# Second expert layer: deeper lead of transposes and first products, and one PSUM bank and one rectifying engine per tile

## Chip, cores, metric

One core of a Trainium2 chip runs the whole program. The metric is the device time of one execution in microseconds (us); lower is better. The kernel before takes 1164.05 us (median of three runs, 1163.82 to 1165.67).

## What is computed

A small language tower in fp32: token embedding and value embedding of 8 x 500 tokens (width 128), then two layers, each a mixer (a long convolution, then an attention) followed by a mixture of experts. The change touches the expert layers, the second one above all. Its reference, cut to the core:

```python
h = h + _L1_ffn_ref(_layernorm(h), g1, g2, W1, b1, W2, b2)

def _L1_ffn_ref(x, g1, g2, W1, b1, W2, b2):     # x: 4000 tokens x 128
    # two groups of 8, then two experts of 8 in each: four of 64 experts for a token
    # c1, c2: softmax weights of the picks
    h = relu(einsum('td,gedh->tgeh', xt, W1) + b1)      # 128 -> 256
    y = einsum('tgeh,gehd->tged', h, W2) + b2           # 256 -> 128
    out = sum over the picks of c1 * c2 * y
```

The first expert layer is of the same form with 8 experts, two picks for a token and a middle layer of 512.

## The kernel before

**Routing.** Only the picked experts are computed. Token rows are sorted by expert and cut into blocks of 128. A table on the chip names, for each tile of work, a block and an expert; a block that holds rows of several experts is worked several times. The second layer (`FFN[1]`, `c.n == 1`) has 125 blocks, 64 experts and so 188 tiles; the first (`c.n == 0`) has 63 blocks and 70 tiles. The program is written out for all tiles, with expert numbers and places of blocks read from the table into registers (`Words`, a load for every two tiles, line 420).

**A tile** has these steps, each on one engine, tied by semaphores that count up:

- POOL gathers the 128 rows of a block from DRAM into one of eight places (`RING`), line 871. Gather j waits until block j - 8 has been transposed (`turned`). There are 125 gathers, one for a block.
- PE transposes the block (`turn`, line 634) into bank `u % 2` of PSUM; DVE copies it to SBUF (line 507, semaphore `blocks_in`).
- DVE copies the tile's expert weights and bias from `big` into one of four places (`stage`, line 504, semaphore `w1_ready`).
- PE makes the first products (`first`, line 639): two chunks (`HC` = 2) of 128 columns. Chunk 0 goes to bank 2 + u % 2, chunk 1 to bank 4 + u % 2.
- ACT rectifies chunk 0 (line 606), DVE chunk 1 (line 512), both into `hid[u % 2]`.
- PE makes the second products (`second`, line 646) into bank 6 + u % 2 once both semaphores, `hid_dve` and `hid_act`, are there.
- ACT copies the result out (line 624), SP stores two tiles at a time to DRAM (line 481).

**Order on PE** in iteration u: transpose of u + 2, first products of u + 1, second products of u. Transposes stop after block 124; from then on the blocks are in SBUF and an iteration holds products only. On DVE: copy of transpose u + 2, rectify u + 1, stage weights of u + 3. On ACT: rectify u + 1, copy result u. PE's waits in an iteration with a transpose are the row's landing, `blocks_in`, `hid_dve` and `hid_act`; without a transpose they are `w1_ready`, `hid_dve` and `hid_act`, and once in eight tiles (line 675) `blocks_in` as well. Every fp32 matmul shows in the trace as two, so four MATMUL records stand for the two products of a step.

**Around it.** POOL has two more sets of gathers, of result rows that are added up for each token. The first 32 (line 884) may start before the layer's end: after DVE has worked out, at tile 156 (`stores_needed`, lines 533 to 541, in front of it `lower_places` at tile 144), how many stores they need, and after those stores have landed. The other 96 (line 949) wait for all results (`results_in`, line 494); from the ninth on each waits for an addition by DVE (line 1309), which in turn follows the late gates (lines 1227 to 1245), eight bias products (lines 2149 and 2156) and the bias's addition (line 998).

Of the kernel before, what the change touches and what calls it, by code (L numbers as in the profile page):

```python
# [25 lines left out]
D = 128  # L26
# [15 lines left out]
class Ffn:  # L42


    def __init__(self, n, groups, experts, picks, hidden, wide, w1, b1, w2, b2):
# [6 lines left out]
        self.full = (self.blocks - 2) // RING  # L52
# [80 lines left out]
def tower_kernel(nc, a, out):  # L133
# [15 lines left out]
    with ExitStack() as ctx:  # L149
# [200 lines left out]
        class Ring:  # L350

            def __init__(self, c):
# [10 lines left out]
                self.rows, self.hid = take(RING, 128), take(2, 128 * c.HC)  # L363
                self.res = take(RING, 128)
# [85 lines left out]

        def store_rows(sp, c):

            sp.wait_ge(S(f"x{c.n + 1}_act"), B if c.n else B // 2)
            if c.n == 0:
                sp.wait_ge(S("x1_dve"), B // 2)
            for lo, hi in ((0, 112), (112, R)):
                sp.dma_start(xrows[:, :].rearrange("(p t) d -> p (t d)", p=R)[lo:hi], xbuf[lo:hi, :]).then_inc(S(f"x{c.n + 1}_st"), 16)

        def expert_dma(sp, c):
# [31 lines left out]
            sp.wait_ge(S(p + "w1_ready"), c.tiles + 5)  # L491
            sp.wait_ge(S(p + "hid_dve"), c.tiles + 3)
            sp.wait_ge(S(p + "hid_act"), c.tiles + 3)
            sp.sem_inc(S(p + "results_in"), 1)  # L494

        def expert_vector(dve, c, me):
# [3 lines left out]
            half = c.HC // 2  # L500
# [5 lines left out]
            def turn(u, kept):  # L506
                v.tensor_copy(ring.blocks[:, bass.ds(kept, 128)], ps[:, u % 2, 0:128]).then_inc(S(p + "blocks_in"), 1)  # L507

            def rectify(u):
                w = ring.w1[u % U]  # L510
                for k in range(half, c.HC):
                    last = v.tensor_scalar(ring.hid[u % 2][:, 128 * k:128 * k + 128], ps[:, 4 + u % 2, 128 * k:128 * k + 128],  # L512
# [45 lines left out]
            dve.sem_inc(S(p + "hid_dve"), 2)  # L558
            dve.wait_ge(S(f"w{c.n}_ld"), 16 * weight_loads(c))
            w1, _ = pairs_of(mybir.EngineType.DVE, stage_table, 0, 2, (c.E - 1) * c.wcols, (KEEP[c.n] - 1) * 128)  # L560
            words = Words(dve, p, stage_table, 2, (c.E - 1) * c.wcols, (KEEP[c.n] - 1) * 128)
            dve.wait_ge(S("bank_filled"), nfill[at[f"holder{c.n}", 0]])
            stage(0, 0)
            dve.wait_ge(S(p + "turned"), 1)
            v.tensor_copy(ring.blocks[:, 0:128], ps[:, 0, 0:128]).then_inc(S(p + "blocks_in"), 1)
            stage(w1[0], 1)
            dve.wait_ge(S(p + "turned"), 2)
            v.tensor_copy(ring.blocks[:, 128:256], ps[:, 1, 0:128]).then_inc(S(p + "blocks_in"), 1)
            stage(w1[1], 2)
            dve.wait_ge(S(p + "hid_filled"), 3)  # L570
            rectify(0)

            def tiles(first_tile, count, turns):
# [17 lines left out]
            tiles(c.full * RING, RING, c.blocks - 2 - c.full * RING)  # L591
# [6 lines left out]
        def expert_scalar(act, c):  # L598

            p, ring, s = f"f{c.n}_", Ring(c), nc.scalar  # L600
            half, hid = c.HC // 2, 128 * c.HC

            def rectify(u):
                w = ring.w1[u % U]
                for k in range(half):
                    last = s.activation(ring.hid[u % 2][:, 128 * k:128 * k + 128], ps[:, 2 + u % 2, 128 * k:128 * k + 128],  # L606
                                        ACT.Relu, bias=w[:, hid + k:hid + k + 1])
                last.then_inc(S(p + "hid_act"), 1)
            act.sem_inc(S(p + "hid_act"), 2)
# [7 lines left out]
            def tiles(first_tile, count):  # L617
                for u in range(count):
                    act.wait_ge(S(p + "hid_filled"), first_tile + (u + 4))
                    rectify(u + 1)  # L620
# [8 lines left out]
        def expert_tensor(pe, c):  # L629
# [3 lines left out]
            def turn(u):  # L633
                t.transpose(ps[:, u % 2, 0:128], ring.rows[u % RING], ident).then_inc(S(p + "turned"), 1)  # L634

            def first(u, kept):
                turned = ring.blocks[:, bass.ds(kept, 128)]
                for k in range(c.HC):
                    last = t.matmul(ps[:, (2 if k < c.HC // 2 else 4) + u % 2, 128 * k:128 * k + 128], ring.w1[u % U][:, 128 * k:128 * k + 128],  # L639
                                    turned, start=True, stop=True)  # L640
                last.then_inc(S(p + "hid_filled"), 1)

            def second(w2, u):
                w = w2v[:, bass.ds(w2, c.HC * D)]
                for k in range(c.HC):
                    last = t.matmul(ps[:, 6 + u % 2, 0:D], ring.hid[u % 2][:, 128 * k:128 * k + 128],  # L646
# [3 lines left out]
            words = Words(pe, p, tile_table, 0, (c.E - 1) * c.HC * D, (KEEP[c.n] - 1) * 128)  # L650
            pe.sem_inc(S(p + "hid_filled"), 2)
            pe.sem_inc(S(p + "res_filled"), 2)
            pe.wait_ge(S("row_ld0"), 16 + earlier_rows(c, 0))
            turn(0)
            pe.wait_ge(S("row_ld1"), 16 + earlier_rows(c, 1))
            turn(1)
            pe.wait_ge(S(p + "w1_ready"), 3)
            pe.wait_ge(S(p + "blocks_in"), 1)
            first(0, 0)
# [3 lines left out]
            def tiles(first_tile, count, turns):  # L663
# [1551 lines left out]
```

## Time and profile before

| what | value |
|---|---|
| median of 3 runs | 1164.05 us |
| span of the profiled execution, first to last instruction | 1254.4 us |
| PE busy | 737.2 us (59%) |
| DVE busy | 748.9 us (60%) |
| ACT busy | 406.2 us (32%) |
| POOL busy | 536.2 us (43%) |
| granted TensorE clock, mean | 0.721 of 2.4 GHz |

The profiled execution's own time is told by its span alone; it is 90 us longer than the median of the runs, so not every stretch of the trace lasts as long in a run as it does here. A row of the page's groups or of a stretch's groups gives line, engine, operation, tiles, count, busy time and mean of one, and after the bar the idle time ahead of it with what ended it. A row of the timeline gives start, length, engine, line, operation, count and in brackets the idle time before it. A row of windows gives busy time and count (x) of each engine, the granted clock, DMA share and GB/s.

### The profile page before, as it was taken

Reading aid. Unit: us, or ns where it says so; the run is one execution under the profiler, and the core shown is the slowest. Engines: PE = TensorE matmul, PEld = TensorE weight load, DVE = VectorE, ACT = ScalarE, POOL = GpSimd, SP = SyncE. Lnnn points to the kernel's source line nnn. Section 1 sums busy time; section 2 is a strip of 40 time slices with the busy share of each in tenths; the row PEclk is TensorE's granted clock in tenths of the full one; section 3 lists DMA queues with packets and bytes.
Section 4 is the critical chain, followed back from the end, with each engine's and each line's share of the span. In section 5 each row is a group of like instructions: output and inputs, shape, how many; then the busy total and the mean of one; then the engine's idle time right before and its main releaser. Section 6 shows DMA issues by size and latency. Waiting matters only on the chain.

```text
span 1254.4 us, 16064 instructions
## 1 busy us (share of the span) xinstructions
PE 737.2 (59%) x4622; PEld 585.6 (47%) x4622; DVE 748.9 (60%) x2175; ACT 406.2 (32%) x1123; POOL 536.2 (43%) x562
## 2 busy tenths in 40 slices
PE   0205966669999237878597413577777894452000
PEld 0205355559999214434255401366666894442000
DVE  6896174856666318788776799555555552275222
ACT  2274151524444133433102306533333462220000
POOL 8853000245450645563100005756666306347664
PEclk9657975559999656676665655589999997665555
DMA  2390049502221266657500404033333222112221
GB/s 67 113 388 1 1 143 320 173 24 68 71 72 42 58 119 127 142 124 137 94 0 1 129 0 138 23 83 85 88 86 88 77 64 66 53 43 77 63 54 52
DMA packets 113503, 111.45 MB, mean 89 GB/s; under 512 B 15891, under 2 KB 99922, under 8 KB 113170
## 3 DMA queue, kind: packets, MB, share of 16 engines
q1 hardware_dynamic: 100172, 83.36, 24.5%
q0 software_dynamic: 13248, 27.06, 8.4%
q8 instruction: 42, 0.69, 0.2%
q14 instruction: 41, 0.34, 0.1%
HBM read 76.08 MB, written 34.26 MB: 88 GB/s over the span
## 4 chain that ended last, share of the span: by engine, by line
PE 46%; DVE 30%; issue 10%; another core or an unknown queue 6%; ACT 3%; DMA 2%; POOL 1%; SPq 1%; DVEq 0%; ACTq 0%; POOLq 0%
PE ps L639 13%; PE ps L646 12%; DVE wide L1330 6%; DVE h L1309 5%; PE ps L1896 4%; PE ps L634 2%; DVE bnst L964 2%; DVE wide L1208 2%; PE ps L2066 2%; PE ps L2107 2%; PE ps L2156 1%; ACT wide L1694 1%; PE ps L2046 1%; DVE mv L967 1%
## 5 line engine op out<-in xcount | busy, mean ns | idle before, releaser
L871 POOL DMA_INDIRECT wide<-xrows,holder x188 | 180.1, 958 | 137.5 <-PE ps L634 91.1
L639 PE MATMUL ps<-wide 128*128 (+1 forms) x1324 | 205.9, 288 | 42.6 <-issue 25.4
L646 PE MATMUL ps<-big,wide 128*128 x1312 | 196.2, 282 | 40.3 <-issue 21.7
L639 PEld LDWEIGHTS ps<-wide 128*128 128x128 f32 x1324 | 174.7, 198 | 56.2 <-issue 53.3
L646 PEld LDWEIGHTS ps<-big,wide 128*128 128x128 f32 x1312 | 171.8, 196 | 43.7 <-issue 43.6
L512 DVE TENSOR_SCALAR wide<-ps,wide 128x128 f32<-128x128 f32 x331 | 109.2, 348 | 129.5 <-PE ps L639 78.6
L1330 DVE TENSOR_REDUCE wide<-ps 125x3 f32<-125x1500 f32 (+1 forms) x96 | 143.7, 1540 | 46.4 <-PE ps L1896 44.4
L606 ACT ACTIVATE wide<-ps,wide 128x128 f32<-128x128 f32 x331 | 114.0, 366 | 169.8 <-PE ps L639 132.9
L1896 PE MATMUL ps<-big 97*125 97x500 bf16 x256 | 105.4, 548 | 40.3 <-DVE wide L1330 33.0
L949 POOL DMA_INDIRECT wide<-results,place x96 | 95.8, 998 | 68.2 <-SPq L494 26.8
L862 POOL TENSOR_SCALAR wide<-tileno,sm 125x128 f16<-125x128 f16 x64 | 40.8, 644 | 168.4 <-DVE sm L1195 143.9
L624 ACT COPY wide<-ps 128x128 f32<-128x128 f32 x258 | 68.4, 265 | 114.9 <-PE ps L646 82.2
L507 DVE COPY wide<-ps 128x128 f32 x184 | 53.4, 290 | 80.2 <-PE ps L634 67.6
L504 DVE COPY wide<-big 128x258 f32 (+2 forms) x264 | 87.0, 330 | 3.9 <-issue 3.8
L905 POOL DMA_INDIRECT wide<-results,place x64 | 61.0, 954 | 60.6 <-SPq L494 34.3
L1896 PEld LDWEIGHTS ps<-big 97*125 97x125 bf16 x256 | 42.9, 193 | 88.6 <-DVE wide L1330 51.2
L2156 PE MATMUL ps<-b,cst 8*125 8x128 f32 (+1 forms) x128 | 33.0, 435 | 75.4 <-issue 70.5
L1309 DVE SCALAR_TENSOR_TENSOR h<-wide,big,h 125x128 f32<-125x128 f32 x96 | 32.7, 351 | 74.6 <-DVE h L1309 24.7
L2156 PEld LDWEIGHTS ps<-b,cst 8*125 8x125 f32 (+1 forms) x128 | 28.3, 322 | 81.3 <-issue 72.3
L2046 PE MATMUL ps<-cst,wide 125*128 125x125 f32 x96 | 22.4, 390 | 62.8 <-ACT wide L1694 62.7
L634 PE MATMUL ps<-cst,wide 128*128 128x128 f32 x188 | 53.4, 285 | 7.2 <-DMA wide<-xrows,holder 4.6
L884 POOL DMA_INDIRECT big<-results,place x32 | 30.4, 950 | 58.5 <-DMA results<-wide 49.1
(384 smaller groups left out, 1197.2 us busy)
## 6 DMA issues: line engine op xcount, KB each, us to landing
results<-wide SPq DMA_DIRECT2D x129, 128.0 KB, 1.8
big<-kappa SPq DMA_DIRECT2D x8, 1750.0 KB, 21.4
big<-parts SPq DMA_DIRECT2D x96, 125.0 KB
big<-in_L_ffn_W_dram SPq DMA_DIRECT2D x10, 1024.0 KB, 9.6
big<-in_L_ffn_W_dram SPq DMA_DIRECT2D x64, 128.0 KB, 2.7
parts<-wide SPq DMA_DIRECT2D x24, 250.0 KB
xrows<-wide SPq DMA_DIRECT2D x2, 1792.0 KB
wide<-xrows,holder POOLq DMA_INDIRECT x188
```

The lines of the kernel that those rows point to most:

```text
L504: v.tensor_copy(ring.w1[u % U], w1v[:, bass.ds(w1, c.wcols)]).then_inc(S(p + "w1_ready"), 1)
L512: last = v.tensor_scalar(ring.hid[u % 2][:, 128 * k:128 * k + 128], ps[:, 4 + u % 2, 128 * k:128 * k + 128], w[:, hid + k:hid + k + 1], 0. ...
L606: last = s.activation(ring.hid[u % 2][:, 128 * k:128 * k + 128], ps[:, 2 + u % 2, 128 * k:128 * k + 128], ACT.Relu, bias=w[:, hid + k:hid ...
L634: t.transpose(ps[:, u % 2, 0:128], ring.rows[u % RING], ident).then_inc(S(p + "turned"), 1)
L639: last = t.matmul(ps[:, (2 if k < c.HC // 2 else 4) + u % 2, 128 * k:128 * k + 128], ring.w1[u % U][:, 128 * k:128 * k + 128], turned, sta ...
L646: last = t.matmul(ps[:, 6 + u % 2, 0:D], ring.hid[u % 2][:, 128 * k:128 * k + 128], w[:, D * k:D * k + D], start=k == 0, stop=k == c.HC - 1)
L871: gp.indirect_dma_start(ring.rows[j % RING], None, xrows[:, :], bass.IndirectOffsetOnAxis(ap=holder[:, j:j + 1], axis=0)).then_inc(S(f"row ...
L949: gp.indirect_dma_start(got[m % 8], None, results[f][:, :], bass.IndirectOffsetOnAxis(ap=place[f][:, k, t:t + 1], axis=0)).then_inc(S(f"go ...
L1309: v.scalar_tensor_tensor(h[:, t, :], rows[0:R, :], swapped_gate[:, k, t:t + 1], h[:, t, :], ALU.mult, ALU.add).then_inc(S("f1_combined"), 1)
L1330: v.tensor_reduce(out=mcol[:, j, H * b + lo:H * b + hi], in_=ps[0:R, 3 * (n % 2):3 * (n % 2) + hi - lo, 0:L], axis=AX.X, op=ALU.max).then_ ...
L1896: last = t.matmul(ps[0:R, 3 * (n % 2) + head - lo, 0:L], stack[0:SROWS, 0, b % 2, head, R * j:R * j + R], stack[0:SROWS, 1, b % 2, head, : ...
L2156: last = t.matmul(p[0:R, D * j:D * j + D], cT[0:c.E, R * j:R * j + R], b2[0:c.E, f, :], start=True, stop=True)
```

## The change

For the second layer alone (`c.n == 1`; the first keeps its numbers):

- transposes run four tiles ahead instead of two (`lead`), first products two instead of one (`ahead`), staged weights five instead of three (`stages`, still four places, so DVE waits for the rectification of tile u + 1 before it stages u + 5);
- a tile's two chunks go to one bank, 2 + u % 4, and are rectified by one engine: ACT for even tiles, DVE for odd ones, into four places instead of two;
- PE waits for one rectification semaphore instead of two, and in addition for `res_ready` (the result copy two tiles back) and, in each iteration, for `blocks_in` and `w1_ready`;
- in the first layer PE waits for `blocks_in` and `w1_ready` in each iteration.

```diff
+        self.ahead = 2 if n else 1
+        self.lead = 4 if n else 2
+        self.stages = 5 if n else 3
+        self.slots = 4 if n else 2
...
+                if c.n:
+                    self.hid += [cst[:, 128 + 256 * i:384 + 256 * i] for i in range(2)]
...
+        def middle(c, u, k):
+            n = 2 + u % 4 if c.n else (2 if k < c.HC // 2 else 4) + u % 2
+            return ps[:, n, 128 * k:128 * k + 128]
+
+        def halves(c, u, engine):
+            if c.n:
+                return range(c.HC) if engine == ("act", "dve")[u % 2] else range(0)
+            return range(c.HC // 2) if engine == "act" else range(c.HC // 2, c.HC)
...
+        def wait_rectified(eng, c, u):
+            for engine in (("act", "dve")[u % 2],) if c.n else ("dve", "act"):
+                eng.wait_ge(S(f"f{c.n}_hid_{engine}"), rectified(c, u, engine))
...
                     if u < turns:
-                        dve.wait_ge(S(p + "turned"), first_tile + (u + 3))
-                        turn(u, words.value(u, 1))
-                    dve.wait_ge(S(p + "hid_filled"), first_tile + (u + 4))
-                    rectify(u + 1)
-                    stage(words.value(u, 0), u + 3)
+                        dve.wait_ge(S(p + "turned"), first_tile + (u + c.lead + 1))
+                        turn(u + c.lead, words.value(u, 1))
+                    if first_tile + u + c.ahead < c.tiles and halves(c, u + c.ahead, "dve"):
+                        dve.wait_ge(S(p + "hid_filled"), first_tile + (u + c.ahead + 3))
+                        rectify(u + c.ahead)
+                    if first_tile + u + c.stages < c.tiles:
+                        if c.stages > U:
+                            wait_rectified(dve, c, first_tile + u + c.stages - U)
+                        stage(words.value(u, 0), u + c.stages)
...
                 for u in range(count):
+                    n = u + c.lead
+                    if c.n and first_tile + u + c.ahead < c.tiles:
+                        pe.wait_ge(S(p + "blocks_in"), min(first_tile + (u + c.ahead + 1), c.blocks))
                     if u < turns:
-                        pe.wait_ge(S(f"row_ld{(u + 2) % RING}"), (first_tile + (u + 2) // RING * RING) * (16 // RING) + 16 + earlier_rows(c, u + 2))
-                        turn(u + 2)
-                        pe.wait_ge(S(p + "blocks_in"), first_tile + (u + 2))
-                    if u >= turns:
-                        pe.wait_ge(S(p + "w1_ready"), first_tile + (u + 4))
-                    if u == turns:
-                        pe.wait_ge(S(p + "blocks_in"), c.blocks)
-                    first(u + 1, words.value(u, 1))
-                    pe.wait_ge(S(p + "hid_dve"), first_tile + (u + 3))
-                    pe.wait_ge(S(p + "hid_act"), first_tile + (u + 3))
+                        pe.wait_ge(S(f"row_ld{n % RING}"), (first_tile + n // RING * RING) * (16 // RING) + 16 + earlier_rows(c, n))
+                        turn(n)
+                    if first_tile + u + c.ahead < c.tiles:
+                        if c.n == 0:
+                            pe.wait_ge(S(p + "blocks_in"), min(first_tile + (u + c.ahead + 1), c.blocks))
+                        pe.wait_ge(S(p + "w1_ready"), first_tile + (u + c.ahead + 3))
+                        first(u + c.ahead, words.value(u, 1))
+                    wait_rectified(pe, c, first_tile + u)
+                    if c.n:
+                        pe.wait_ge(S(p + "res_ready"), first_tile + (u + 1))
                     second(words.value(u, 0), u)
```

## Rows read from the trace of the kernel before

**Rows 1.** The page's first line: span and instructions.
```profile
span 1254.4 us, 16064 instructions
```
**Rows 2.** Windows: busy time and count of PE, PEld, DVE, ACT, POOL; clock, DMA.
```profile
300.00:400.00 100.00, 100.00 (x899) 100.00 (x898) 64.52 (x209) 47.02 (x159) 39.66 (x43) 1.00 0.23 65
...
823.00:1003.00 180.00, 137.72 (x1087) 126.68 (x1087) 96.34 (x360) 69.91 (x242) 104.95 (x110) 0.99 0.31 85
1003.00:1041.00 38.00, 37.09 (x290) 33.80 (x288) 22.75 (x92) 22.51 (x72) 0.00 (x0) 1.00 0.22 64
...
1107.00:1244.00 137.00, 24.37 (x96) 18.50 (x96) 55.17 (x136) 4.55 (x8) 94.96 (x96) 0.51 0.22 58
```
**Rows 3.** Timeline beside gathers, 883 to 886 us, cut.
```profile
883.17 0.61 PE L646 MATMUL ps<-big,wide 128*128 x4
...
885.62 0.27 ACT L624 COPY wide<-ps 128x128 f32<-128x128 f32 x1 [1.08 <-PE ps L646]
885.75 0.29 DVE L507 COPY wide<-ps 128x128 f32 x1 [0.88 <-PE ps L634]
```
**Rows 4.** Timeline of POOL: four row gathers one after another.
```profile
881.32 0.94 POOL L871 DMA_INDIRECT wide<-xrows,holder  x1 [1.15 <-PE ps L634]
882.56 0.94 POOL L871 DMA_INDIRECT wide<-xrows,holder  x1 [0.30 <-issue]
883.81 0.94 POOL L871 DMA_INDIRECT wide<-xrows,holder  x1 [0.30 <-issue]
885.88 0.94 POOL L871 DMA_INDIRECT wide<-xrows,holder  x1 [1.14 <-PE ps L634]
```
**Rows 5.** Line 634 from 803 to 1003 us: duration min/median/max, first and last start.
```profile
L634 PE MATMUL ps<-cst,wide x125: 272/273/476, 803.6 to 998.6; 128*128 128x128 f32 x125
```
**Rows 6.** Timeline, the last row gather, and two late transposes.
```profile
991.05 0.95 POOL L871 DMA_INDIRECT wide<-xrows,holder  x1 [1.23 <-remote]
...
997.58 0.27 PE L634 MATMUL ps<-cst,wide 128*128 128x128 f32 x1
...
998.58 0.27 PE L634 MATMUL ps<-cst,wide 128*128 128x128 f32 x1
```
**Rows 7.** Timeline, 1041 to 1088 us, cut: engines that wait beside result gathers.
```profile
1075.80 0.27 ACT L624 COPY wide<-ps 128x128 f32<-128x128 f32 x1 [9.45 <-remote]
...
1084.20 0.35 DVE L512 TENSOR_SCALAR wide<-ps,wide 128x128 f32<-128x128 f32 x1 [17.68 <-remote]
```
**Rows 8.** Lines from 830 to 990 us: DVE's three operations of a tile.
```profile
L512 DVE TENSOR_SCALAR wide<-ps,wide 128x128 f32<-128x128 f32 x104 | 36.2, 348 | 16.7 <-PE ps L639 11.3 <-issue 1.8
L504 DVE COPY wide<-big 128x258 f32 x104 | 30.8, 296 | 0.1
L507 DVE COPY wide<-ps 128x128 f32 x104 | 30.2, 290 | 60.3 <-PE ps L634 53.8 <-issue 4.0 <-remote 0.7
```
**Rows 9.** Timeline after the transposes: four second products in a row.
```profile
1010.23 0.64 PE L646 MATMUL ps<-big,wide 128*128 x4
...
1011.35 0.61 PE L646 MATMUL ps<-big,wide 128*128 x4
...
1012.24 0.64 PE L646 MATMUL ps<-big,wide 128*128 x4
...
1013.47 0.61 PE L646 MATMUL ps<-big,wide 128*128 x4
```
**Rows 10.** Line 481 to 1037.5 us: stores of two tiles, first and last issue.
```profile
L481 SPq DMA_DIRECT2D results<-wide x79: 359/360/367, 817.6 to 1037.0; - x79
```
**Rows 11.** Timeline: first of the 32 early result gathers.
```profile
1041.04 0.95 POOL L884 DMA_INDIRECT big<-results,place  x1 [49.05 <-DMA results<-wide]
```
**Rows 12.** Timeline after the layer: late gates, first and ninth of the last gathers.
```profile
1105.38 1.95 DVE L1227 TENSOR_TENSOR wide<-sm,em 125x512 f32<-125x512 f32 x4
...
1107.73 1.15 POOL L949 DMA_INDIRECT wide<-results,place  x1 [26.84 <-SPq L494]
...
1124.69 1.00 POOL L949 DMA_INDIRECT wide<-results,place  x1 [3.90 <-DVE h L1309]
```

More of the change, by code:

```diff
@@ L449, in late_place, with turned_at, rectified, wait_all_rectified @@
             return 16 * (m // 8) + 8 + m % 8 if m < 8 * EARLY else 8 * EARLY + m
+        def turned_at(u):
+            return ps[:, u % 2, 0:128]
+        def middle(c, u, k):
[5 more added lines that the diff above has]
+            return range(c.HC // 2) if engine == "act" else range(c.HC // 2, c.HC)
+        def rectified(c, u, engine):
+            return u // 2 + 1 if c.n else u + 3
+        def wait_rectified(eng, c, u):
+            for engine in (("act", "dve")[u % 2],) if c.n else ("dve", "act"):
+                eng.wait_ge(S(f"f{c.n}_hid_{engine}"), rectified(c, u, engine))
+        def wait_all_rectified(eng, c):
+            for u in range(c.tiles - 2, c.tiles) if c.n else (c.tiles - 1,):
+                wait_rectified(eng, c, u)
         def store_rows(sp, c):
@@ L506, in turn @@
             def turn(u, kept):
-                v.tensor_copy(ring.blocks[:, bass.ds(kept, 128)], ps[:, u % 2, 0:128]).then_inc(S(p + "blocks_in"), 1)
+                v.tensor_copy(ring.blocks[:, bass.ds(kept, 128)], turned_at(u)).then_inc(S(p + "blocks_in"), 1)
             def rectify(u):
                 w = ring.w1[u % U]
-                for k in range(half, c.HC):
-                    last = v.tensor_scalar(ring.hid[u % 2][:, 128 * k:128 * k + 128], ps[:, 4 + u % 2, 128 * k:128 * k + 128],
+                for k in halves(c, u, "dve"):
+                    last = v.tensor_scalar(ring.hid[u % c.slots][:, 128 * k:128 * k + 128], middle(c, u, k),
                                            w[:, hid + k:hid + k + 1], 0.0, ALU.add, ALU.max)
@@ L590, in expert_vector @@
                 tiles(i * RING, RING, RING)
-            tiles(c.full * RING, RING, c.blocks - 2 - c.full * RING)
+            tiles(c.full * RING, RING, c.blocks - c.lead - c.full * RING)
             if c.tiles // RING > c.full + 1:
@@ L618, in tiles @@
                 for u in range(count):
-                    act.wait_ge(S(p + "hid_filled"), first_tile + (u + 4))
-                    rectify(u + 1)
+                    if first_tile + u + c.ahead < c.tiles and halves(c, u + c.ahead, "act"):
+                        act.wait_ge(S(p + "hid_filled"), first_tile + (u + c.ahead + 3))
+                        rectify(u + c.ahead)
                     act.wait_ge(S(p + "res_filled"), first_tile + (u + 3))
@@ L633, in turn @@
             def turn(u):
-                t.transpose(ps[:, u % 2, 0:128], ring.rows[u % RING], ident).then_inc(S(p + "turned"), 1)
+                t.transpose(turned_at(u), ring.rows[u % RING], ident).then_inc(S(p + "turned"), 1)
             def first(u, kept):
@@ L638, in first @@
                 for k in range(c.HC):
-                    last = t.matmul(ps[:, (2 if k < c.HC // 2 else 4) + u % 2, 128 * k:128 * k + 128], ring.w1[u % U][:, 128 * k:128 * k + 128],
-                                    turned, start=True, stop=True)
+                    last = t.matmul(middle(c, u, k), ring.w1[u % U][:, 128 * k:128 * k + 128], turned, start=True, stop=True)
                 last.then_inc(S(p + "hid_filled"), 1)
@@ L645, in second @@
                 for k in range(c.HC):
-                    last = t.matmul(ps[:, 6 + u % 2, 0:D], ring.hid[u % 2][:, 128 * k:128 * k + 128],
+                    last = t.matmul(ps[:, 6 + u % 2, 0:D], ring.hid[u % c.slots][:, 128 * k:128 * k + 128],
                                     w[:, D * k:D * k + D], start=k == 0, stop=k == c.HC - 1)
                 last.then_inc(S(p + "res_filled"), 1)
-            words = Words(pe, p, tile_table, 0, (c.E - 1) * c.HC * D, (KEEP[c.n] - 1) * 128)
+            if c.ahead > 1:
+                _, kept = pairs_of(mybir.EngineType.PE, tile_table, 0, c.ahead - 1, (c.E - 1) * c.HC * D, (KEEP[c.n] - 1) * 128)
+            words = Words(pe, p, tile_table, c.ahead - 1, (c.E - 1) * c.HC * D, (KEEP[c.n] - 1) * 128)
             pe.sem_inc(S(p + "hid_filled"), 2)
             pe.sem_inc(S(p + "res_filled"), 2)
[L653 to L659, printed above, removed]
+            for u in range(c.lead):
+                pe.wait_ge(S(f"row_ld{u}"), 16 + earlier_rows(c, u))
+                if u >= 2:
+                    pe.wait_ge(S(p + "blocks_in"), u - 1)
+                turn(u)
+            for u in range(c.ahead):
+                pe.wait_ge(S(p + "w1_ready"), u + 3)
+                pe.wait_ge(S(p + "blocks_in"), u + 1)
+                first(u, kept[u - 1] if u else 0)
             if c.n:
@@ L683, in expert_tensor @@
                 tiles(i * RING, RING, RING)
-            tiles(c.full * RING, RING, c.blocks - 2 - c.full * RING)
+            tiles(c.full * RING, RING, c.blocks - c.lead - c.full * RING)
             if c.tiles // RING > c.full + 1:
@@ L880, in _ @@
                     pool.wait_ge(S("early_known"), 2)
-                    pool.wait_ge(S(q + "w1_ready"), LOWER_AT + 6)
+                    pool.wait_ge(S(q + "w1_ready"), LOWER_AT + c.stages + 3)
                     for b in range(EARLY):
@@ L2182, in _ @@
                 pe.wait_ge(S(q + "res_ready"), c.tiles + 2)
[L2183 to L2184 removed]
+                wait_all_rectified(pe, c)
                 if f == 0:
```

50 lines of the change are left out of this document (27 added, 23 removed).

## The prediction

> **What bounds the kernel now.** I read the page first, then windows over the stages, then the timeline of the second expert layer engine by engine, and POOL's timeline beside it.
>
> The page's span is 90 us longer than the median of the runs [rows 1]; something in the trace isn't in the runs. So the first question is what in this layer is real. In the windows the first expert layer is full: PE is busy for 100 of 100 us [rows 2]. The second isn't: from 823 to 1003 us PE is busy for 137.7 of 180 us [rows 2]. The 125 transposes start over 195 us, 1.57 us apart [rows 5].
>
> The timeline says where that time goes. Second products start at 883.17 us and by their length end at 883.78, but ACT, which waits for nothing else of them, copies their result at 885.62, and DVE gets the next transpose only at 885.75 [rows 3]. Every third tile or so PE's end is told 1.5 to 2 us late while PE goes on issuing. It happens beside gathers: POOL issues three 1.25 us apart, then waits for PE [rows 4]. After the last gather, at 991.05 us, transposes follow each other in 1.00 us with no such hold [rows 6]. And while POOL issues the 32 early result gathers without a pause (from 1041.04 us [rows 11]), ACT waits 9.45 us and DVE 17.68 us for PE [rows 7]. I call these holds.
>
> Are the holds in the runs? Take them out. The transposes then go at the pace of the gathers, 1.25 us, in 125 x 1.25 = 156 us instead of 195: 39 us less. The early gathers then start at 1041 - 39 = 1002 us, take 32 x 1.25 = 40 us and end at 1042. The layer's last 28 tiles take 1105.4 - 1041.0 = 64 us in the trace against 28 x 1.02 = 29 us without holds [rows 9, 11, 12], so it ends before POOL is through, and the 26.8 us for which POOL waits at 1107.73 us [rows 12] go too. Together 66 us of the 90 that the trace is too long. I therefore take the holds as things of the profiled execution. The Trainium skill, "NOTIFIC — the notification-queue block", section 7.1, says that the block's internal pipeline always presses back on its producers rather than lose a record, which would let recording throttle an engine; rows 3 and 7 look like that, and no row proves it.
>
> So in a run the layer is bound by POOL: row gathers at 1.25 us, PE with about 1.0 us of work in each of them [rows 4, 6]. After the last gather PE has the rest to do at 1.02 us a tile. The 32 early gathers start when the stores of their tiles have landed: the 79th store, tiles 156 and 157, is issued at 1037.0 us and POOL starts at 1041.04 [rows 10, 11]. From there POOL's 32 + 96 gathers lead to the end: in the last stretch POOL is busy for 95 of 137 us, with pauses of 0.30 us between [rows 2]. What the change does counts up to tile 157's store.
>
> **The change part by part.**
>
> *Deeper lead while rows are gathered.* Nothing. Tile 1.25 us, PE 1.0 us, DVE 0.290 + 0.348 + 0.296 = 0.93 us [rows 8] on average, also when it rectifies both chunks of every second tile. The new waits add at most 0.11 us a tile on PE (below), 1.11 < 1.25. Cover: the gather. If the gather were faster than 1.11 us, PE would bound both kernels and the waits would cost up to 0.06 x 120 = 7 us.
>
> *The lead itself costs at the end of the gathers.* The order on PE is fixed: transpose u + 4, first products u + 2, second products u. When transpose 124 arrives, the kernel before stands at second products 122, the new one at 120. Both get it at the same time, so 2 tiles more lie behind it: 2 x 1.02 = +2.0 us.
>
> *More waits on PE's queue after the transposes.* Before, an iteration there has `w1_ready` and two waits for the rectified halves; once in eight tiles `blocks_in` is added. Second products start at 1010.23, 1011.35, 1012.24 and 1013.47 us: 1.12, 0.89 and 1.23 us [rows 9]. The long ones hold the load of registers for two tiles (line 420), after which PE starts its next product late; the 1.23 is the tile with the added wait for `blocks_in`. One wait more right behind a register load costs 0.11 us; in the other tile of a pair it is hidden, 0.89 being eight matmuls without a gap. The new kernel has that wait in each iteration (the wait for `res_ready` takes the place of one for a half). So 3 of 4 pairs become 0.11 us longer: 0.041 us a tile, over 37 tiles (120 to 157) +1.5 us. Queued behind each such wait are the first products of u + 2, and behind them everything on PE. Bounds: 0, if two waits share an instruction, and 0.11 x 37 = +4.1 us.
>
> *What the lead saves there.* The pattern gives (3 x 2.01 + 2.12)/8 = 1.02 us a tile. The window 1003 to 1041 us has 290 matmul records, 36.3 tiles, in 38 us: 1.05 us [rows 2]. The excess, about 1.0 us, holds DVE's side work at tiles 144 and 156, for which PE waits; a lead of two tiles covers a part. I take -0.7 us; bounds -1.4 and 0.
>
> *One bank and one engine for a tile.* Rectification of a tile takes 0.70 us instead of 0.35, off the path: between first products u and second products u lie more than a tile and a half of PE work, 1.5 us. DVE's new wait, for tile u + 1's rectification before it stages u + 5, has behind it that copy and the next transpose's copy; ACT has been through with u + 1 for a tile. 0 us; bounds 0 and +1.
>
> *Start of the layer.* First products wait for four transposes instead of two, 2.5 us at 1.25 us a row. The eight places for rows give POOL room until its ninth gather, 10 us in, so POOL is not held. 0 us; bounds 0 and +2.5.
>
> *First layer.* `w1_ready` is waited for in each iteration. PE is busy for 100 of 100 us [rows 2], register loads included, so its queue runs ahead by more than a wait. 0 us; bound 0.11 x 35 pairs = +3.9 us.
>
> *Registers and end of the layer.* Some loads more at the start, three weight copies of DVE less at the end: nothing. Behind tile 157 the new kernel's slower tiles are covered by the early gathers. The ninth last gather follows the late gates by 1124.69 - 1105.38 = 19.3 us [rows 12]; without holds the layer ends at about 1105.4 - 39 - 35 = 1031, so that chain is at 1051, and POOL at 1042 + 8 x 1.25 = 1052. A margin of 1 to 3 us, from which the slower tiles could add another 28 x 0.041 = 1.1 us.
>
> Sum: 2.0 + 1.5 - 0.7 = +2.8 us. Against the profiled execution's own time that is 1254.4 + 2.8; but there the holds are, and a longer lead hides them, so its span may well fall. The runs don't have them, so I add to their median: 1164.05 + 2.8 = 1166.9 us.
>
> **The rivals.**
>
> *A: the holds are in the runs as well.* For it: they are what the rows show. Against it: the 66 of 90 us above. Three tiles take 4.6 us [rows 4]; a tile more in flight lets PE work 1.0 us longer through each hold, down to the gathers' 3 x 1.25 = 3.75 us. Gain 0.85 us in each of 40 groups, 34 us: 1130. If a fifth of them is real, 7 - 3 = 4 us: 1160. This decides if a fifth or more of the excess in the transposes' stretch is real.
>
> *B: no difference.* The waits share instructions or the queue hides them, DVE's side work is covered, and the 2.0 us of the lead are partly won back since PE can make up the lag in tiles where it now waits: 1164 to 1166.
>
> *C: PE is held by its queue.* If gathers in a run take 1.1 us or less, PE's waits bind among the transposes too, and show in the first layer: 2.8 + 3 to 7 us: 1170 to 1174. It decides from a gather pace below 1.11 us. Against it: with 253 gathers of this layer 0.14 us faster, the runs would be 35 us shorter than I make them.
>
> **How the numbers follow.** A measurement tells about 0.2%, 2.3 us, from no change. My forecast (+1 to +4.5 us around +2.8) has 0.60, of which 0.38 lies above 2.3 us; B 0.15; A 0.17, 0.05 for the full gain and 0.12 for a fifth or so, of which 0.01 falls within 2.3 us; C 0.08, nearly all above. That makes faster 0.16, same 0.38, slower 0.46. The likeliest is the forecast, 1166.9. Range: 1158 to 1171.5, which leaves out A's full gain with a bit of its small one, and half of C. It is wide below, as a share of holds weighs more than any other cost.
>
> **What would show it.** In the new kernel's trace: transposes' starts 1.25 us apart or more and the holds still there beside gathers; the stretch after the last gather with pairs of second products of 2.12 us instead of 2.01; 68 second products behind the last transpose instead of 66; DVE never late for its stagings. I would be wrong if the runs fell by 5 us or more (A), if pairs became shorter than 2.01 us after the transposes, or if PE's share in the first layer fell below 100 of 100.

## The result, and the profile after

The changed kernel takes 1168.92 us (median of 13 runs, 1163.59 to 1173.58) against 1164.05 for the kernel before (13 runs, 1161.38 to 1167.03): ratio 1.0043, 95% interval 1.003 to 1.0056. That is +4.9 us; the forecast was +2.8.

One thing must be known to read the numbers: the kernel before has two levels, which differ between the chips on which the comparisons ran. On one of them all 29 runs of the kernel before took 1256 to 1266 us, near the 1254.4 us of the profile shown ahead of the prediction; on the others they took 1159 to 1168. So each time below stands beside that of the kernel before on its own chip, and for a trace of before at the lower level I profiled the kernel before again (first experiment).

The page's first line, after:

```profile
span 1166.3 us, 16260 instructions
```

Windows of after (columns as in [rows 2]): first layer, the stretch from the last transpose to the 79th store, and the late gathers:

```profile
300.00:400.00 100.00, 100.00 (x899) 100.00 (x898) 64.19 (x208) 47.16 (x159) 38.57 (x41) 1.00 0.23 64
...
944.40:989.20 44.80, 39.43 (x308) 35.69 (x309) 22.45 (x93) 20.06 (x77) 0.00 (x0) 1.00 0.20 57
...
1036.00:1156.00 120.00, 21.00 (x84) 15.91 (x82) 48.49 (x134) 3.98 (x7) 90.74 (x97) 0.50 0.25 67
```

The clock is at its upper level, 2.4 GHz (1.00), in the whole stretch that changed. Two lines fix that stretch: the 125 transposes and the 79 stores that the early gathers wait for, each with first and last start. After, and below them the first early gather:

```profile
L674 PE MATMUL ps<-cst,wide x125: 272/299/476, 788.9 to 944.4; 128*128 128x128 f32 x125
L510 SPq DMA_DIRECT2D results<-wide x79: 359/359/367, 796.9 to 989.2; - x79
...
991.90 0.95 POOL L930 DMA_INDIRECT big<-results,place  x1 [50.47 <-DVE wide L531]
```

The same of the kernel before at the lower level:

```profile
L634 PE MATMUL ps<-cst,wide x125: 272/273/476, 786.2 to 942.8; 128*128 128x128 f32 x125
L481 SPq DMA_DIRECT2D results<-wide x79: 359/360/367, 793.1 to 981.3; - x79
...
985.38 0.94 POOL L884 DMA_INDIRECT big<-results,place  x1 [44.47 <-DVE wide L504]
```

The whole difference of the two spans, 1166.3 - 1159.7 = 6.6 us, can be read here. The last transpose starts 1.6 us later (944.4 against 942.8). From it to the 79th store it is 44.8 us instead of 38.5: +6.3. From the store to the first early gather, 2.7 instead of 4.1: -1.4. From there to the end, 174.4 instead of 174.3: +0.1. So the change is in one stretch, in which PE works alone. I call it the lead-out, and it is a better measure than the time, since in the three kernels profiled twice it repeats within 0.1 us:

| kernel | lead-out, us | time, us | before, same chip | ratio and 95% interval |
|---|---|---|---|---|
| before | 38.5 | | | |
| after | 44.8 | 1168.92 | 1164.05 | 1.0043 [1.003, 1.0056] |
| after, again | 44.8 | 1171.96 | 1165.48 | 1.0054 [1.0039, 1.007] |
| aligned | 35.1 | 1160.09 | 1163.79 | 0.9966 [0.9949, 0.9982] |
| aligned, again | 35.1 | 1161.72 | 1165.48 | 0.9963 [0.9948, 0.9977] |
| aligned, fewer waits | 35.1 | 1159.20 | 1163.79 | 0.9956 [0.9938, 0.9973] |
| before, table 8 bytes on | 49.1 | 1189.65 | 1163.79 | 1.0206 [1.018, 1.0232] |
| before, table 16 bytes on | 38.5 | 1257.61 | 1260.25 | 0.9979 [0.9964, 0.9994] |
| before, more waits | 40.2 | 1262.28 | 1260.25 | 1.0011 [0.9994, 1.0027] |
| one tile ahead | 41.3 | 1265.45 | 1260.25 | 1.0048 [1.0032, 1.0064] |
| aligned, lead 3, stagings 5 | 34.5 | 1252.45 | 1260.25 | 0.9942 [0.9926, 0.9957] |
| lead 3, stagings 4 | 37.6 | 1164.24 | 1165.48 | 0.9982 [0.9967, 0.9998] |
| the same, fewer waits | 35.4 | 1158.75 | 1165.48 | 0.9952 [0.9936, 0.9968] |

What fills the lead-out? PE's timeline of after, second products on L685:

```profile
970.32 0.71 PE L679 MATMUL ps<-wide 128*128 x4 [0.31 <-issue]
970.86 0.61 PE L685 MATMUL ps<-big,cst 128*128 x4
971.31 0.61 PE L679 MATMUL ps<-wide 128*128 x4
971.76 0.61 PE L685 MATMUL ps<-big,cst 128*128 x4
972.65 0.71 PE L679 MATMUL ps<-wide 128*128 x4 [0.28 <-issue]
```

A pair of tiles takes 972.65 - 970.32 = 2.33 us, where four products back to back (0.45 us each) would take 1.79. The gap stands once a pair, behind the second of its two second products, and no other engine is named for it ("issue"). What the code has there, once a pair, is the load of four words from the tile table into PE's registers. Its line in the trace, after (L426, PE's queue and DVE's; then PE's in the first layer), shows it:

```profile
L426 PEldq TENSOR_LOAD <-tile_table x88: 997/1040/1207, 800.1 to 1013.8; - x88
L426 DVEq TENSOR_LOAD <-stage_table x86: 341/346/354, 800.9 to 1009.9; - x86
...
L426 PEldq TENSOR_LOAD <-tile_table x35: 327/332/527, 271.4 to 392.9; - x35
```

and before:

```profile
L420 PEldq TENSOR_LOAD <-tile_table x86: 327/332/376, 801.0 to 1003.6; - x86
```

PE's load takes 1.04 us where it took 0.33; DVE's and the first layer's are unchanged. The load is the same four words. What the diff does to it: `Words` gets `c.ahead - 1` = 1 as its first index instead of 0, and the table is written one pair of words further on, so each of PE's loads in the second layer starts 8 bytes further. Places are counted here from the start of the table; where the table itself lies in memory no trace tells.

### The profile page after: what moved, and what is told of

The parts are those of the page before. It is cut to its first block, busy times and chain, and to the rows that moved or that the text cites. A ratio compares the mean times of both kernels' runs of the same rounds, so it can differ in the third digit from the quotient of the medians.

```text
span 1166.3 us, 16260 instructions
## 1 busy us (share of the span) xinstructions
PE 726.1 (62%) x4610; PEld 574.6 (49%) x4610; DVE 748.1 (64%) x2166; ACT 391.2 (34%) x1120; POOL 536.7 (46%) x562
## 4 chain that ended last, share of the span: by engine, by line
PE 43%; DVE 28%; POOL 10%; issue 7%; DMA 7%; ACT 4%; SPq 1%; DVEq 0%; POOLq 0%; ACTq 0%
PE ps L679 11%; PE ps L685 10%; DVE wide L1376 7%; POOL wide L995 4%; PE ps L1942 4%; DMA wide<-results,place 3%; POOL big L930 3%; DVE bnst L1010 3%; DVE wide L1254 3%; PE ps L2112 3%; PE ps L674 2%; ACT wide L1740 2%; PE ps L2153 2%; POOL wide L917 2%; PE ps L2202 1%
## 5 line engine op out<-in xcount | busy, mean ns | idle before, releaser
L679 PE MATMUL ps<-wide 128*128 (+1 forms) x1312 | 200.0, 285 | 9.2 <-issue 8.5
L679 PEld LDWEIGHTS ps<-wide 128*128 128x128 f32 x1312 | 169.5, 194 | 16.1 <-issue 15.1
L685 PE MATMUL ps<-big,wide 128*128 x936 | 131.9, 276 | 0.0
L685 PEld LDWEIGHTS ps<-big,wide 128*128 128x128 f32 x936 | 118.2, 193 | 0.2 <-issue 0.2
L644 ACT ACTIVATE wide<-ps,wide 128x128 f32<-128x128 f32 x234 | 73.1, 363 | 114.5 <-PE ps L679 113.7
L539 DVE TENSOR_SCALAR wide<-ps,wide 128x128 f32<-128x128 f32 x234 | 71.4, 347 | 62.1 <-PE ps L679 60.5
L995 POOL DMA_INDIRECT wide<-results,place x96 | 91.3, 951 | 29.3 <-issue 24.4
L531 DVE COPY wide<-big 128x258 f32 (+3 forms) x258 | 84.5, 335 | 4.1 <-issue 4.0
L951 POOL DMA_INDIRECT wide<-results,place x64 | 60.8, 949 | 50.7 <-SPq L522 33.7
L685 PE MATMUL ps<-big,cst 128*128 x376 | 57.4, 275 | 0.2 <-issue 0.2
L2213 PE MATMUL ps<-wide 125*128 125x128 f16 x192 | 28.5, 303 | 41.3 <-DVE wide L1254 39.7
```

The costliest lines, as they stand in the source:

```text
L531: v.tensor_copy(ring.w1[u % U], w1v[:, bass.ds(w1, c.wcols)]).then_inc(S(p + "w1_ready"), 1)
L539: last = v.tensor_scalar(ring.hid[u % c.slots][:, 128 * k:128 * k + 128], middle(c, u, k), w[:, hid + k:hid + k + 1], 0.0, ALU.add, ALU.max)
L644: last = s.activation(ring.hid[u % c.slots][:, 128 * k:128 * k + 128], middle(c, u, k), ACT.Relu, bias=w[:, hid + k:hid + k + 1])
L679: last = t.matmul(middle(c, u, k), ring.w1[u % U][:, 128 * k:128 * k + 128], turned, start=True, stop=True)
L685: last = t.matmul(ps[:, 6 + u % 2, 0:D], ring.hid[u % c.slots][:, 128 * k:128 * k + 128], w[:, D * k:D * k + D], start=k == 0, stop=k == c ...
L995: gp.indirect_dma_start(got[m % 8], None, results[f][:, :], bass.IndirectOffsetOnAxis(ap=place[f][:, k, t:t + 1], axis=0)).then_inc(S(f"go ...
```

## The experiments

**First comparison: what is in the runs, and is it the place of the load?** The kernel before, unchanged.

> The kernel before, profiled once more, unchanged. If the long holds of PE's ends beside gathers belong to that one profiled execution, this one has none: span about 1162 us, row gathers 1.25 us apart from first to last (156 us), pairs of second products 2.01 us after the last transpose, the early result gathers starting about 39 us earlier against the last row gather than in the first trace. If the holds belong to the kernel and only the change took them away, the span is again about 1254 us.

Measured: 1161.5 us, span 1159.7, transposes 1.26 us apart, no holds. Its gathers, to compare with [rows 4]:

```profile
879.31 0.94 POOL L871 DMA_INDIRECT wide<-xrows,holder  x1 [0.30 <-issue]
880.56 0.94 POOL L871 DMA_INDIRECT wide<-xrows,holder  x1 [0.30 <-issue]
881.80 1.00 POOL L871 DMA_INDIRECT wide<-xrows,holder  x1 [0.30 <-issue]
```

Against the 1254.4 us shown ahead, the transposes' stretch is 38.4 us shorter (156.6 instead of 195.0), the first transpose 17.4 us earlier, the lead-out the same (38.5 and 38.4), the rest 39.0 us shorter.

*aligned*: the changed kernel with the second layer's tile table 8 bytes further on, so that PE's loads start where they did.

```diff
-tile_table = sb("tile_table", [1, 2 * TAB], I32)
+tile_words = sb("tile_table", [1, 2 * TAB], I32)
+tile_tables = [tile_words[:, 0:2 * TAB], tile_words[:, 2:2 * TAB]]
...
-words = Words(pe, p, tile_table, c.ahead - 1, ...)
+words = Words(pe, p, tile_tables[c.n], c.ahead - 1, ...)
```

> The changed kernel with the second layer's table of tiles moved by one pair of words (8 bytes), so that each of PE's loads of four words starts where it did in the kernel before; nothing else differs. Theory place (the load is slow because the change moved its first word by 8 bytes): loads of registers on PE take 0.33 us instead of 1.0, pairs of second products after the last transpose 2.12 us instead of 2.34, over 37 tiles 4.0 us less, about 1165 us, 0.1% over the kernel before. Theory queue (the load waits for products queued before it, since the longer lead lets PE's queue run further ahead): loads still 1.0 us, pairs 2.34 us, 1169 us, 0.4% over.

Measured: 1160.09 us, 3.7 under before; more than I expected, since the pairs are not 2.12 us but 1.79. Load, lead-out window and timeline:

```profile
L427 PEldq TENSOR_LOAD <-tile_table x87: 327/332/561, 801.8 to 996.3; - x87
...
942.90:978.00 35.10, 35.10 (x314) 34.75 (x313) 21.96 (x92) 20.11 (x77) 0.00 (x0) 1.00 0.26 73
...
960.45 0.61 PE L686 MATMUL ps<-big,cst 128*128 x4
960.89 0.61 PE L680 MATMUL ps<-wide 128*128 x4
961.34 0.61 PE L686 MATMUL ps<-big,wide 128*128 x4
961.79 0.61 PE L680 MATMUL ps<-wide 128*128 x4
```

PE is busy for 35.10 of 35.10 us: a load of 0.33 us is hidden wholly behind queued matmuls. By my sum the waits should have shown here; they don't.

*before_shifted*: the same shift in the kernel before, alone.

> The kernel before with the second layer's table of tiles moved by one pair of words (8 bytes), nothing else. Theory place: loads of registers on PE take 1.0 us instead of 0.33 and pairs after the last transpose grow from 2.01 to 2.3 us or more, over 35 tiles 5 us or more: 1169 us, 0.4% over the kernel before or more; among the row gathers nothing changes, as 1.25 us a tile still covers it. Theory queue: loads stay at 0.33 us and the time at 1164 us.

Measured: 1189.65 us, +25.9, five times the least that I expected.

```profile
L421 PEldq TENSOR_LOAD <-tile_table x87: 996/1000/1008, 800.8 to 1038.5; - x87
...
L635 PE MATMUL ps<-cst,wide x125: 272/299/447, 791.3 to 962.8; 128*128 128x128 f32 x125
...
882.38 0.30 PE L635 MATMUL ps<-cst,wide 128*128 128x128 f32 x1 [0.58 <-issue]
...
885.15 0.30 PE L635 MATMUL ps<-cst,wide 128*128 128x128 f32 x1 [0.49 <-issue]
```

The load is at 1.00 us again, with nothing else changed: place, not lead or waits, makes it slow. My expectation counted only the lead-out, and too little there: it rises by 10.6 us, since pairs take 2.68 us (987.45 - 984.77) and not 2.3. And among the row gathers a pair now takes 885.15 - 882.38 = 2.77 us, more than its two gathers' 2.50, so PE and not POOL bounds the layer: transposes 171.5/124 = 1.38 us apart instead of 1.26, +14.9 us. Together 25.5. The changed kernel escapes this, its transposes still 155.5/124 = 1.25 us apart.

*aligned_fewer_waits*: aligned, with `blocks_in` not waited for behind the last transpose.

```diff
-if c.n and first_tile + u + c.ahead < c.tiles:
+if c.n and first_tile + u + c.ahead < c.blocks + 1:
     pe.wait_ge(S(p + "blocks_in"), ...)
```

> The kernel of run aligned without PE's wait for blocks_in in iterations that need no block later than the last. My term for that wait is 0.11 us for each pair of tiles: pairs go from 2.12 us to 2.01 us, over 34 tiles 1.9 us less than run aligned, about 1163 us. If two waits cost PE no more than one, it is the same as run aligned.

Measured: lead-out 35.1 us, the same; 1159.20 us, its interval overlaps aligned's. With a load of 0.33 us and this lead the wait costs nothing.

**Second comparison: control, and the parts one by one** (the chip with the upper level). *before_shifted16*: the table 16 bytes on instead of 8.

> The kernel before with the second layer's tile table moved by 16 bytes instead of 8, so that each of PE's register loads (four words, 16 bytes) starts at a multiple of 16 bytes again. Control for the 8-byte shift, which gave 1189.65 us and loads of 1.0 us. Theory (the place within 16 bytes decides): loads of 0.33 us, pairs of second products 2.01 us behind the last transpose, 1161 to 1166 us, no difference from before. Rival (any moved or newly routed table makes the load slow, for instance by what else lies near it): loads of 1.0 us, pairs 2.7 us, 1189 us.

```profile
L421 PEldq TENSOR_LOAD <-tile_table x18: 327/332/334, 999.7 to 1035.7; - x18
...
L635 PE MATMUL ps<-cst,wide x125: 272/273/474, 802.3 to 998.1; 128*128 128x128 f32 x125
L482 SPq DMA_DIRECT2D results<-wide x79: 359/360/367, 817.0 to 1036.6; - x79
```

Load 0.33 us, lead-out 38.5: as before. Moving the table costs nothing; moving it by half a load's 16 bytes does. (The expected 1161 to 1166 us was for the lower level; here it is 1257.61 against 1260.25. The interval of the ratio, up to 0.9994, just leaves out no difference; the lead-out doesn't show these 2.6 us, and I have no cause for them.)

*before_more_waits*: the kernel before with `blocks_in` waited for in each iteration behind the last transpose.

```diff
-if u == turns:
+if u == turns or c.n and u > turns:
     pe.wait_ge(S(p + "blocks_in"), c.blocks)
```

> The kernel before with the wait for blocks_in in every iteration behind the last transpose, where it has it once in eight; register loads stay at their place. This measures the term of my forecast by itself. The forecast's reading: 0.11 us in each of 3 of 4 pairs, pairs 2.12 instead of 2.01 us, second products of tiles 122 to 157 in 36.9 + 13 x 0.11 = 38.3 us, time +1.5 us, 1165.5. Rival (the wait is free, as with the deeper lead): pairs 2.01 and the time of before within 0.5 us.

```profile
L634 PE MATMUL ps<-cst,wide x125: 272/273/473, 800.1 to 996.1; 128*128 128x128 f32 x125
L481 SPq DMA_DIRECT2D results<-wide x79: 359/359/367, 811.2 to 1036.3; - x79
...
1005.35 0.61 PE L646 MATMUL ps<-big,wide 128*128 x4
...
1007.48 0.61 PE L646 MATMUL ps<-big,wide 128*128 x4
```

A pair takes 2.13 us, the lead-out 40.2: +1.7 where the forecast's term was +1.5. The time's interval (-0.8 to +3.4 us) can't tell. So the term is right for the kernel from whose rows it was read, and only for that.

*one_ahead*: the changed kernel's banks and turns, the lead undone.

```diff
-self.ahead = 2 if n else 1
-self.lead = 4 if n else 2
-self.stages = 5 if n else 3
+self.ahead = 1
+self.lead = 2
+self.stages = 3
```

> The changed kernel's banks and its one engine per tile, with the lead undone: first products one tile ahead, transposes two ahead, three stagings, as before. PE's first index is 0 again, so its register loads start at a multiple of 16 bytes and should take 0.33 us. This is the other part of the change alone. Theory (the lead of two tiles is what hides the register load, since PE's queue can run ahead only as far as its waits are met): without it a tile's rectification, 0.70 us instead of 0.35, stands within the 0.89 us between its first and second products, the queue can run less far ahead, and pairs take 2.1 to 2.4 us instead of 2.01; second products of tiles 122 to 157 in 38 to 42 us, 1166 to 1171 us. Rival (banks and turns are what shorten the tiles, the lead costs only its two tiles of lag): pairs 1.78 us, 0.89 a tile, no lag, 1157 us.

```profile
L675 PE MATMUL ps<-cst,wide x125: 272/300/477, 805.9 to 1003.9; 128*128 128x128 f32 x125
L510 SPq DMA_DIRECT2D results<-wide x79: 359/360/367, 819.2 to 1045.2; - x79
...
1020.37 0.61 PE L686 MATMUL ps<-big,wide 128*128 x4
1020.82 0.61 PE L680 MATMUL ps<-wide 128*128 x4
1021.33 0.71 PE L686 MATMUL ps<-big,wide 128*128 x4
1022.08 0.71 PE L680 MATMUL ps<-wide 128*128 x4
1022.63 0.61 PE L686 MATMUL ps<-big,cst 128*128 x4
...
L426 DVEq TENSOR_LOAD <-stage_table x18: 434/622/632, 1005.1 to 1043.7; - x18
```

A pair takes 2.26 us, the lead-out 41.3, and the time rises by 5.2 us, as the first theory said. PE's loads are at 0.33 us. (DVE's take 0.62 us here, though their place within 16 bytes is that of the kernel before.) 1.7 of the +2.8 us is the wait, which this kernel has as well; 1.1 is what banks and turns cost without the lead: there is a gap in each tile now (second products start 0.96 and 1.30 us apart instead of 0.89 and 1.12). The trace of all engines fits a late rectification: the two chunks on DVE end at 1021.18 us, and the second products, due at 1021.27 behind the first ones, start at 1021.33. That it costs the 1.1 us is argued, not shown.

*aligned_lead3*: transposes three ahead, one number changed. The stagings stay five ahead, so DVE takes the place of the next tile for each turned block and first products read other rows; the amount and order of work are the same, but what it computes isn't the layer's result. It serves for its times alone.

> The aligned version with transposes three tiles ahead instead of four, first products still two ahead. Behind the last transpose stands one tile less. Theory (each tile of lead costs one tile at the end of the gathers, and nothing before it, since DVE and PE have 0.3 us and more to spare in each gather): tile 157's second products come 33.6 us behind the last transpose instead of 34.5, time 0.9 us less than aligned, 1159.2 us. Rival (the transposes' copy by DVE is late for the first products when only one tile lies between them): gathers' pace stays 1.25 but tiles behind it get gaps of 0.1 to 0.2 us, no gain or up to +2 us, 1160 to 1162.

```profile
L675 PE MATMUL ps<-cst,wide x125: 272/302/476, 803.6 to 999.8; 128*128 128x128 f32 x125
L511 SPq DMA_DIRECT2D results<-wide x79: 359/360/367, 818.4 to 1034.3; - x79
```

Lead-out 34.5 us, 0.6 less than aligned for one tile less of lead (0.9 expected). The lead-outs of two chips are compared here, since those of the kernel before agree on both. Time 7.8 us under before; aligned wasn't run on that chip, so I draw nothing more from the time. This trace also speaks on rival A: its lead is deeper than that of the kernel before, yet its transposes stand 196.2/124 = 1.58 us apart, as before_more_waits' do (196.0/124). POOL's gathers in before_more_waits:

```profile
880.64 0.94 POOL L871 DMA_INDIRECT wide<-xrows,holder  x1 [0.30 <-issue]
882.76 0.94 POOL L871 DMA_INDIRECT wide<-xrows,holder  x1 [1.17 <-PE ps L634]
884.00 0.95 POOL L871 DMA_INDIRECT wide<-xrows,holder  x1 [0.31 <-issue]
885.25 0.95 POOL L871 DMA_INDIRECT wide<-xrows,holder  x1 [0.30 <-issue]
```

The hold of [rows 4] is there, every third gather. It is there in aligned_lead3 too (883.28 and 887.95 us, waits of 1.15 and 1.14 us), so a lead of three tiles doesn't bridge it.

**Third comparison: does it repeat, and is a shorter lead better?** The changed kernel and aligned again, unedited.

> The changed kernel unedited, beside the kernel before on the chip that this comparison gets. The runs so far show two levels of the kernel before: 1164 us, and 1260 us with PE's ends told late beside gathers, in all 29 runs of one comparison. Theory (what the change costs lies behind the last transpose, where nothing is held): pairs of second products 2.34 us, tile 157's second products 44 us behind the last transpose, +4.9 us at either level, ratio 1.004. Rival A of the forecast (a deeper lead lets PE work through a hold), only at the upper level: transposes 1.27 us apart instead of 1.58, 1225 to 1250 us there.

> The changed kernel with its register loads at a multiple of 16 bytes, once more, beside the two shorter leads on the same chip. Theory: 4 us under the kernel before at either level (1160 or 1256), 34.5 us from the last transpose to tile 157's second products. Rival (the gain of 3.7 us was this one chip's): within 1 us of before.

Measured: 1.0054 and 0.9963, lead-outs 44.8 and 35.1 us, at the lower level. Between the two on one chip lie 10.2 us, 9.7 of them in the lead-out. Rival A at the upper level was not tried with the changed kernel itself.

*lead3*: transposes three ahead with the stagings four ahead, DVE's table moved by 8 bytes as well, so that its loads stay at a multiple of 16.

```diff
-self.lead = 4 if n else 2
-self.stages = 5 if n else 3
+self.lead = 3 if n else 2
+self.stages = 4 if n else 3
```

> The aligned version with transposes three tiles ahead and four stagings (its tables laid out for that, so that each transpose goes to its own place). Theory (each tile of lead costs one tile at the end of the gathers and nothing before it): 33.6 us from the last transpose to tile 157's second products instead of 34.5, and 0.9 us less than aligned in the same comparison. Rival (a fourth tile of lead pays for itself while rows are gathered, or staging one tile later makes PE wait for DVE): the last transpose later by 1 us or more, or gaps of 0.1 us and more in the 0.89 us tiles; same time as aligned or above.

> The three-tile lead without the wait for blocks_in behind the last transpose. Theory (with the two-tile lead of first products that wait is hidden behind matmuls, while in the kernel before it cost 0.15 us a pair): same time as lead3 within 1 us, tiles of 0.89 us. Rival (the wait costs 0.11 us in three of four pairs): 1.5 us less than lead3.

```profile
L677 PE MATMUL ps<-cst,wide x125: 272/296/477, 791.4 to 947.7; 128*128 128x128 f32 x125
L512 SPq DMA_DIRECT2D results<-wide x79: 359/359/367, 800.3 to 985.3; - x79
...
966.15 0.61 PE L688 MATMUL ps<-big,cst 128*128 x4
966.67 0.71 PE L682 MATMUL ps<-wide 128*128 x4
...
968.11 0.61 PE L688 MATMUL ps<-big,wide 128*128 x4
```

PE's loads in the two lead-outs, lead3 and then lead3_fewer_waits:

```profile
L428 PEldq TENSOR_LOAD <-tile_table x19: 332/587/606, 948.2 to 983.9; - x19
...
L428 PEldq TENSOR_LOAD <-tile_table x19: 328/342/610, 943.0 to 976.7; - x19
```

Both expectations missed. lead3's lead-out is 37.6 us where 0.9 less than aligned's 35.1 was expected: pairs take 968.11 - 966.15 = 1.96 us with a gap behind the load. Without the wait it is 35.4. So with the stagings four ahead taking out the same wait gives 2.2 us, where with five it gave nothing. The loads tell how: in lead3 they take 0.59 us, at a place where aligned's take 0.33. The load at 965.81 us ends at 966.40, and the next first products start 0.27 us later, at 966.67.

The same holds in every trace in which a gap stands behind a load. From the load's end to the next first products it is 0.27 us with `blocks_in` and `w1_ready` behind the load, 0.16 with `w1_ready` alone. The difference is the forecast's 0.11 us. What is hidden depends on how early the load starts: 0.28 us before the last matmul of the second products ahead of it with first products one tile ahead (before, one_ahead), 0.76 us with two (after, aligned), 0.64 in lead3 (medians in the lead-outs). With matmuls 0.11 us apart, aligned's 0.33 + 0.27 = 0.60 fits into 0.76 + 0.11; after's 1.02 (its median there) + 0.27 = 1.29 and lead3's 0.59 + 0.27 = 0.86 against 0.64 + 0.11 don't.

With a load of 0.33 us lead3 would have no gap by this sum, so it is the load's length that costs. What makes the load longer stays open. aligned_lead3 (stagings five ahead, transposes three: loads 0.33 us, lead-out 34.5) points to the stagings and not the transposes. But it ran on the other chip and with blocks at other places, and lead3 also moves DVE's table, so this is not shown. The times, 1164.24 and 1158.75, lie 5.5 us apart, more than the 2.2: in the two traces the first transpose alone, which no changed wait touches, starts at 791.4 and 786.2 us. lead3_fewer_waits has the lowest ratio at the lower level, 0.9952, but its interval covers aligned's 0.9963.

## Why the prediction was right, and where it was not

The verdict, slower by more than 0.2%, and the range held. The sum did so partly by luck: two of its terms were far off, with opposite signs.

- *Bound and path*: right. POOL's 1.25 us a gather bounds the layer, the lead-out is what the change moves, and behind the first early gather both kernels need 174.3 and 174.4 us. The early gathers start over 43.5 us in both (985.38 to 1028.90 us in before) and not the 40 that I gave them.
- *Holds*: right for the chip of the comparison, wrong as I put it. They are no thing of one profiled execution: on one chip all 29 runs of before are at 1260 us. Of the 94.7 us between the two traces of before, 38.4 and 39.0 lie where I took out 39 and 27; the other 17.4 lie ahead of the layer's transposes, where I had looked for nothing. What makes the holds stays open. The Trainium skill, "NOTIFIC — the notification-queue block", section 7.1, tells how recording could throttle an engine; no run here shows that it does.
- *Deeper lead while rows are gathered, 0*: right, 1.25 us apart. *First layer, 0*: right, PE 100 of 100 us. *Start of the layer, 0*: right, POOL's 125 gathers start over 155.9 us after and 156.4 before.
- *The lead at the end of the gathers, +2.0*: two tiles of 0.89 would be 1.8; one tile of it measured 0.6 (aligned_lead3).
- *More waits, +1.5*: +1.7 in the kernel before, 0 in aligned. The price was read from a kernel with first products one tile ahead and given to one with two.
- *What the lead saves, -0.7*: this term was mis-sized. From one_ahead to aligned the lead-out falls from 41.3 to 35.1 us, -6.2 with the lead's own cost in it. With a load of 0.33 us the lead covers every gap behind it, not only DVE's side work; I had priced the gap as if it were fixed.
- *One bank and one engine, 0, bound +1*: 1.1 us without the lead; with it PE has no gap left (aligned). A tile's rectification takes 0.61 us, not 0.70.
- *Registers, nothing*: this step failed. I counted the loads and did not look at where they start. Aligned against after is 35.1 against 44.8: +9.7 us. In place of the failed step stands a load of 1.04 us instead of 0.33, once a pair.

The runs' budget of the lead-out, put together from two chips: 38.5 (before) + 2.8 (banks, turns and wait) - 6.2 (lead) + 9.7 (place of the load) = 44.8 us. The forecast had 38.5 + 2.8. The test that I named for it, pairs of 2.12 us, did show the fault: they are 2.33.

## What to carry to other kernels

Where a change moves an index into a table that an engine's queue reads its registers from, look at the start address of each load, not only at their number: a moved first index can cost more than the whole schedule change brings, and padding the table by a pair gives it back. A gap behind a queue instruction has no fixed price: it is what is left once the matmuls queued ahead are through, so a wait or a load costs nothing with enough lead (aligned), and part or all of its length without; take its price from a kernel with the lead that the new one will have, and look at the load's own length there, which can change with the schedule (0.59 us in lead3). And profile the kernel before twice before calling a part of its trace an artefact: here it came back in all runs on another chip.

## What the runs showed of the hardware

- PE's load of four words (16 bytes) into registers takes 1.00 to 1.04 us (medians) where it starts 8 bytes off a multiple of 16 from the table's start (after, before_shifted; none of the 88 and 87 loads shown above under 0.99), and mostly 0.33 us at a multiple of 16, also 16 bytes further. Mostly, since at such a place it took 0.59 us in lead3's lead-out, and DVE's took 0.62 in one_ahead's. Other offsets and sizes were not tried, and why either costs this is not known. The Trainium skill, "DMA: Bandwidth & Descriptors", section "Latency and other measured facts", gives a `tensor_load` a floor of about 600 ns; here 0.33 us was measured, below that floor.
- Where no matmul is queued any more, PE's next one starts 0.16 us after such a load's end with one semaphore wait between them and 0.27 us with two.
- The same program runs at 1164 to 1165 us (medians) in three comparisons and at 1260 us in a fourth, on another chip, at nearly the same mean granted clock (0.732 in before_again, 0.723 and 0.751 in before_shifted16 and before_more_waits at the upper level). In the five traces at the upper level (the four of that comparison and the one ahead of the prediction) every third gather or so on POOL waits for PE; the kernel before's lead-out, which has no gathers, takes 38.4 to 38.5 us at both levels. Whether it is the chip or something else of that comparison stays open.
